# Earlier loads for chunks 2 and 3, zero products in TensorE's waits, products in quarter columns, and results stored by place

## The reference

```
h   = rmsnorm(layernorm(x)) * norm_w;  q, k, v = h Wq, h Wk, h Wv       # 16 heads of 8
lin = causal linear attention, features [1, u, quadratic terms of u],
      u = q Wqf or k Wkf, in chunks of 128 with a running state
win = softmax attention over the key itself and the 64 before it
x1  = x + layernorm(x) + [lin, win] Wout
n   = layernorm(x1);  top 2 of 8 experts by n Wgate + bgate, softmax weights
expert: z = (n W1 + b1)(n W2 + b2);  o = silu(z Wg + bg)(z Wl + bl);  y = o W3 + b3
out = x1 + sum over the token's two experts of weight * y
```

## Time and profile before

| | us |
|---|---|
| median of 3 runs | 412.84 |
| lowest, highest run | 408.07, 413.14 |
| the profiled execution | 410.21 |
| its span, first to last instruction | 408.3 |
| TensorE busy | 343.6 (84%) |
| VectorE busy | 251.6 (62%) |
| GpSimd busy | 219.0 (54%) |
| ScalarE busy | 211.6 (52%) |

### The profile page before, as it was taken

One profiled execution on the slowest core, in us unless ns is written; L12 is line 12 of the kernel. 1 busy time (PEld: TensorE's weight loads), 2 busy tenths in 40 slices (PEclk: granted clock), 3 DMA queues, 4 the chain that ended last, 5 costly groups with the idle time before them and its releaser, 6 DMA issues.

```text
span 408.3 us, 15626 instructions
## 1 busy us (share of the span) xinstructions
PE 343.6 (84%) x5603; PEld 298.1 (73%) x5603; DVE 251.6 (62%) x1001; ACT 211.6 (52%) x574; POOL 219.0 (54%) x368
## 2 busy tenths in 40 slices
PE   0768795699999999999999941699999999999920
PEld 0345584588878788888888830599999999999910
DVE  4665553268986688888887747255555555555515
ACT  0465563366565766676667620355555555555410
POOL 5363554155666577767765554012666655666510
PEclk9999999699999999999999985599999999999985
DMA  7746886878887877554342000223333333333028
GB/s 197 196 123 115 141 218 149 99 166 180 182 188 177 170 134 133 135 128 92 80 92 63 18 32 28 73 60 120 118 122 125 120 127 134 114 119 119 18 67 244
DMA packets 91966, 50.20 MB, mean 123 GB/s; under 512 B 56874, under 2 KB 86220, under 8 KB 91890
## 3 DMA queue, kind: packets, MB, share of 16 engines
q1 hardware_dynamic: 88898, 44.48, 46.0%
q0 software_dynamic: 2272, 4.46, 3.4%
q10 hardware_dynamic: 720, 0.26, 0.3%
HBM read 29.52 MB, written 11.98 MB: 102 GB/s over the span
## 4 chain that ended last, share of the span: by engine, by line
PE 73%; SPq 9%; DMA 6%; DVE 4%; issue 4%; ACT 2%; POOL 1%; DVEq 0%; POOLq 0%; ACTq 0%
PE ps L748 8%; PE ps L754 8%; PE ps L642 6%; PE ps L589 5%; PE ps L720 5%; PE ps L723 4%; PE ps L731 4%; PE ps L638 4%; PE ps L688 4%; PE ps L681 4%; PE ps L601 3%; PE ps L608 3%; SPq L382 3%; SPq L368 3%; PE ps L664 2%
## 5 line engine op out<-in xcount | busy, mean ns | idle before, releaser
L1300 POOL TENSOR_SCALAR_AFFINE_SELECT amat<-amat 128x512 f32<-128x512 f32 x64 | 41.0, 641 | 66.4 <-ACT amat L820 65.7
L1334 POOL DMA_INDIRECT results<-qas,mrowid x39 | 38.2, 979 | 68.1 <-ACT qas L887 68.1
L1103 DVE TENSOR_REDUCE mrow<-ps 128x4 f32<-128x512 f32 x64 | 43.8, 685 | 36.5 <-PE ps L589 36.4
L833 ACT ACTIVATE pmat<-ps 128x512 f32<-128x512 f32 x64 | 38.4, 600 | 54.0 <-PE ps L642 54.0
L1172 DVE SCALAR_TENSOR_TENSOR qas<-ps,bcol,qas 128x128 f32<-128x128 f32 x78 | 26.5, 351 | 34.3 <-ACT qas L893 30.8
L875 ACT ACTIVATE qas<-ps,bcol 128x128 f32<-128x128 f32 x78 | 24.4, 364 | 38.4 <-PE ps L720 38.4
L1182 DVE SCALAR_TENSOR_TENSOR qas<-ps,bcol,qas 128x128 f32<-128x128 f32 x78 | 23.9, 347 | 29.0 <-ACT qas L875 21.7
L820 ACT ACTIVATE amat<-ps 128x512 f32<-128x512 f32 x64 | 38.5, 602 | 1.9 <-PE ps L601 1.7
L1261 POOL DMA_INDIRECT routed<-routed_row,slot x32 | 32.6, 1018 | 12.9 <-issue 5.8
L642 PE MATMUL ps<-minus_ident,mrow 128*128 128x128 bf16 x256 | 36.0, 221 | 0.0
L642 PE MATMUL ps<-minus_ident,mlow 128*128 128x128 bf16 x256 | 35.7, 220 | 0.0
(11 more groups left out here) (170 smaller groups left out, 913.8 us busy)
## 6 DMA issues: line engine op xcount, KB each, us to landing
kv_tok<-w SPq DMA_DIRECT2D x31, 256.0 KB
qa_parts<-wgl SPq DMA_DIRECT2D x12, 256.0 KB, 3.3
ks<-k_parts SPq DMA_DIRECT2D x32, 96.0 KB
qas<-qa_parts SPq DMA_DIRECT2D x32, 96.0 KB
xin<-routed SPq DMA_DIRECT2D x39, 72.0 KB, 1.9
ks<-k_parts SPq DMA_DIRECT2D x32, 64.0 KB
qas<-qa_parts SPq DMA_DIRECT2D x32, 64.0 KB
w<-in_W SPq DMA_DIRECT2D x2, 1024.0 KB
```

The lines of the kernel that those rows point to most:

```text
L833: a_(pmat[:, u % 2].rearrange("p g t -> p (g t)"), ps[:, ST, :], ACT.Exp).then_inc(exp_done, 1)
L1103: v.tensor_reduce(mrow[:, b], ps[:, SQ, :].rearrange("p (a k) -> p a k", k=CH), AX.X, ALU.max).then_inc(max_done, 1)
L1300: q.affine_select(out=amat[:, u % 2], in_=amat[:, u % 2], compare_op=ALU.is_ge, fill=0.0, base=0, pattern=[[0, 4], [1, CH]], channel_multi ...
L1334: q.indirect_dma_start(results, bass.IndirectOffsetOnAxis(mrowid[:, m:m + 1], 0), yw[:, m, :], None, bounds_check=RESULTS - 1, oob_is_err= ...
```

## The change

Stacks 2 and 3 are loaded before the writes of groups 2 and 3: SP's order becomes stack 1, the fill, stack 2, the writes of group 2, stack 3, the writes of group 3, the wait for the writes of groups 1 to 3, stack 4. The weight transfers go out from stack 4 on instead of from stack 3 on.

TensorE gets products of a zeroed buffer `still` with itself, written to a PSUM bank that is then unused: 18 of 512 columns at its start and 4 after the first transposes, 12 and 12 of 128 and 6 and 7 of 512 after the four `post` calls of chunk 16, 6 of 128 and 6 of 512 after the second and third of chunk 17, 30 of 512 before the experts, and 6 of 128 in step -1.

The window scores are made with 32 stationary columns, 16 products a unit. In the experts, ScalarE multiplies b3 by the row's weight into `b3w`, and VectorE multiplies the sum in PSUM by the weight and adds `b3w`. The row numbers of `results` become 16p + c for token p of chunk c, so that a partition's rows lie together, and ScalarE's queue loads the second choice.

```diff
-    vals[:, :, :, 1] = (np.arange(CH)[:, None] + CH * np.arange(NC)[None])[:, :, None] + N * np.arange(TOPK)
+    vals[:, :, :, 1] = (NC * np.arange(CH)[:, None] + np.arange(NC)[None])[:, :, None] + N * np.arange(TOPK)
...
+        BETWEEN = (((12, 128), (12, 128), (6, 512), (7, 512)), ((0, 0), (6, 128), (6, 512), (0, 0)))
+        def half_of_results(k):
+            return results[k * N:(k + 1) * N, :].rearrange("(p c) d -> p c d", p=CH)
...
@@ SP @@
             load_stack(1)
-            for g in range(2, NG):
-                write_parts(g)
             sp.wait_ge(r_in, 16 * N_R)
...
-            for g in range(1, NG):
-                sp.wait_ge(parts_out[g], 16 * WRITES)
...
             for c in range(2, NC):
+                if c == GC:
+                    for g in range(1, NG):
+                        sp.wait_ge(parts_out[g], 16 * WRITES)
                 load_stack(c)
-                for dst, src, got in pieces[c - 3:c - 2] if c >= 3 else ():
+                if c < GC:
+                    write_parts(c)
+                for dst, src, got in pieces[c - GC:c - GC + 1] if c >= GC else ():
                     sp.dma_start(dst, src).then_inc(got, 16)
...
             for g in range(NG):
-                for k in range(2):
-                    lo = k * N + g * GT
-                    sp.dma_start(res[k][:, g * GC:(g + 1) * GC], results[lo:lo + GT, :].rearrange("(c p) d -> p c d", p=CH)).then_inc(res_in[g], 16)
+                sp.dma_start(res[0][:, g * GC:(g + 1) * GC], half_of_results(0)[:, g * GC:(g + 1) * GC]).then_inc(res_in[g], 16)
...
@@ TensorE @@
+            def keep_running(times, cols):
+                for _ in range(times):
+                    mm(ps[:, PHI, 0:cols], still[:, 0:128], still[:, 0:cols], start=True, stop=True)
...
+            pe.wait_ge(still_ready, 1)
+            keep_running(18, 512)
             pe.wait_ge(i_in, 16)
             transposes(0)
+            keep_running(4, 512)
...
@@ window_scores @@
-                    r = WINDOW * (hh % 2)
-                    t = mm(ps[r:r + WINDOW, SQ, (hh // 2) * CH:(hh // 2 + 1) * CH], qs[:, p, h, j * WINDOW:(j + 1) * WINDOW],
-                           ks[:, p, j, h, :], start=True, stop=True)
+                    for z in range(0, WINDOW, 32):
+                        r, at = WINDOW * (hh % 2) + z, j * WINDOW + z
+                        t = mm(ps[r:r + 32, SQ, (hh // 2) * CH:(hh // 2 + 1) * CH], qs[:, p, h, at:at + 32], ks[:, p, j, h, :],
+                               start=True, stop=True)
...
                     post(c, u, c % 2)
+                    keep_running(*BETWEEN[c - NC][u])
...
             pe.wait_ge(r_count, NC)
+            keep_running(30, 512)
             pe.wait_ge(e_in, 16 * N_E)
...
@@ TensorE's step @@
+                if j == -1:
+                    keep_running(6, 128)
...
                     if j > 1:
-                        pe.wait_ge(y_added, j - 1)
+                        pe.wait_ge(y_weighted, j - 1)
...
@@ ScalarE's step @@
-                if on(-1):
-                    m = (k + 3) % 4
-                    act.wait_ge(y_added, j)
-                    act.wait_ge(meta_copied, j)
-                    if j >= 5:
-                        act.wait_ge(y_out[m], 16 * turn(-1))
-                    a_(yw[:, m, :], yb[:, (k + 1) % 2, :], ACT.Copy, scale=mweight[:, m:m + 1]).then_inc(y_weighted, 1)
                 if on(0):
+                    act.wait_ge(meta_copied, j + 1)
+                    if j >= 2:
+                        act.wait_ge(y_weighted, j - 1)
+                    a_(b3w[:, k % 2, :], b3[:, bass.ds(expert(0), 1), :].rearrange("p a f -> p (a f)"), ACT.Copy,
+                       scale=mweight[:, k:k + 1]).then_inc(b3w_ready, 1)
...
@@ ScalarE, at the end @@
+            for k in range(4):
+                act.wait_ge(y_out[k], 16 * ((NT - k + 3) // 4))
+            for g in range(NG):
+                act.dma_start(res[1][:, g * GC:(g + 1) * GC], half_of_results(1)[:, g * GC:(g + 1) * GC]).then_inc(res_in[g], 16)
...
@@ VectorE @@
+            v.memset(still[:], 0.0).then_inc(still_ready, 1)
             v.memset(hT[:, 0:WINDOW], 0.0).then_inc(settled, 1)
...
-                    v.tensor_tensor(yb[:, q, :], ps[:, Y, 0:D], flat(b3[:, bass.ds(expert(-1), 1), :]), ALU.add).then_inc(y_added, 1)
+                    dve.wait_ge(b3w_ready, j)
+                    if j >= 5:
+                        dve.wait_ge(y_out[m], 16 * turn(-1))
+                    v.scalar_tensor_tensor(out=yw[:, m, :], in0=ps[:, Y, 0:D], scalar=mweight[:, m:m + 1], in1=b3w[:, q, :],
+                                           op0=ALU.mult, op1=ALU.add).then_inc(y_weighted, 1)
```

More of the change, by code:

```diff
@@ L230, in build @@
         yw = late2[:, 2560:3072].rearrange("p (a d) -> p a d", a=4)
-        yb = late2[:, 3072:3328].rearrange("p (a d) -> p a d", a=2)
+        b3w = late2[:, 3072:3328].rearrange("p (a d) -> p a d", a=2)
         xin = sb("xin", [CH, 4, ROW])
@@ L237, in build @@
         ps = ctx.enter_context(nc.psum_tensor("ps", [128, 8, 512], F32))
+        still = sb("still", [128, 512], BF16)
         SQ, ST, A, OUT0, OUT1, PHI, KV, TR = range(8)
@@ L244, in build @@
         zeroed = sem("zeroed")
+        still_ready = sem("still_ready")
         wstep, wstep_c = sem("wstep"), sem("wstep_c")
@@ L274, in build @@
         (tx_ready, xT_copied, bcol_ready, x2_ready, x1w_ready, x2_added, z_ready, meta_copied, g_ready, l_ready, silu_done, o_ready,
-         y_ready, y_added, y_weighted) = (sem(n) for n in (
+         y_ready, b3w_ready, y_weighted) = (sem(n) for n in (
              "tx_ready", "xT_copied", "bcol_ready", "x2_ready", "x1w_ready", "x2_added", "z_ready", "meta_copied", "g_ready", "l_ready",
-             "silu_done", "o_ready", "y_ready", "y_added", "y_weighted"))
+             "silu_done", "o_ready", "y_ready", "b3w_ready", "y_weighted"))
         res_in = [sem(f"res_in{g}") for g in range(NG)]
         res_sum, out_sum = sem("res_sum"), sem("out_sum")
+        BETWEEN = (((12, 128), (12, 128), (6, 512), (7, 512)), ((0, 0), (6, 128), (6, 512), (0, 0)))
         TX, X2, X1, G, L, Y = SQ, ST, A, (OUT0, OUT1), (KV, TR), PHI
@@ L893, in step @@
                         a_(sg[:, k % 2, h, :], ps[:, G[h], 0:CH], ACT.Silu, bias=bcol[:, k, 4 + h:5 + h]).then_inc(silu_done, 1)
-            run_steps(act, step)
+            run_steps(act, step, (0,))
+            for k in range(4):
+                act.wait_ge(y_out[k], 16 * ((NT - k + 3) // 4))
+            for g in range(NG):
+                act.dma_start(res[1][:, g * GC:(g + 1) * GC], half_of_results(1)[:, g * GC:(g + 1) * GC]).then_inc(res_in[g], 16)
         @block.vector
@@ L1184, in step @@
                 if on(-1):
-                    q = (k + 1) % 2
+                    m, q = (k + 3) % 4, (k + 1) % 2
                     dve.wait_ge(y_ready, j)
-                    if j > 2:
-                        dve.wait_ge(y_weighted, j - 2)
-                    v.tensor_tensor(yb[:, q, :], ps[:, Y, 0:D], flat(b3[:, bass.ds(expert(-1), 1), :]), ALU.add).then_inc(y_added, 1)
+                    dve.wait_ge(b3w_ready, j)
[3 more added lines that the diff above has]
+                                           op0=ALU.mult, op1=ALU.add).then_inc(y_weighted, 1)
                 if on(1):
```

## The result

| | before | after |
|---|---|---|
| median of 4 runs, us | 412.58 | 406.02 |
| lowest, highest | 408.07, 413.14 | 405.07, 407.34 |
| the profiled execution, its span | 410.21, 408.3 | 405.99, 404.1 |

The account below looks back on a forecast made before the run. TensorE was taken to bound attention and experts, besides idle gaps, half clock, and the head and tail set by other engines and transfers. Terms summed to 19.6: 410.2 - 19.6 = 390.5 us; forecast 386 to 394 (chance 0.60), range 384 to 399.

Parts of the forecast that it names:

- The stacks: SP's queue before attention: the 8.0 us wait and 1.45 at half clock go, a 1.5 us wait comes at chunk 4; -8.0.
- Rival 1: The wait moves: chunk 4 waits some 5 us for its stack, with half clock behind it; 395.5 us, chance 0.17.
- Quarter columns: Window scores in attention: equal strip widths save 0.11 us a unit in 47 units; -5.2 us.
- rivals 2 and 4: 2: each quarter product takes its own slot, 403 us (398.2 at 25 ns), chance 0.06; 4: no overlap, 431, chance 0.03.
- Zeros: Zero products keep TensorE's clock up: -1.7 us at the head, -3.3 after attention, in the first expert tiles.
- Rival 3: Zeros don't hold the clock: no gain at the head or in the experts; 397.5 us, chance 0.08.
- Results of an expert: Experts' weighting moves from ScalarE to VectorE's addition: only the last tile's ScalarE step goes; -0.4 us.
- Results by place: Loading results at the tail in 2 KB instead of 512 B pieces: 6.2 us against 7.4; -1.0 us.

Follow-up runs that it names:

- the wait by group: Changed kernel, but SP waits only for group 1's writes before chunk 4's stack, for groups 2 and 3's behind it; 404.00 us, ratio 0.9826 to the kernel before.
- quarters in two units: Changed kernel with SP's wait for groups 2 and 3 behind chunk 4's stack, and 32-column window scores only in units 0 and 3; 402.04 us, ratio 0.9769.
- the fastest version: Changed kernel with window scores back in 64 columns and SP's wait for groups 2 and 3 behind chunk 4's stack; 400.27 us, again 399.64.

## Why the prediction was wrong, point by point

**The stacks (-8.0).** The wait and its half-clock unit went as summed (the lead grows by 9.7 us from unit 7 to unit 9), and the new wait was 1.8 for my 1.5. That it came so close is partly luck: in the other profiles with this order it was 0, 1.3, 1.4, 2.8 and 3.2. What failed is the rest of that term: the half clock behind the new wait, 1.8 us, and stops of 5.4 instead of 0.8 us. Alone the edit gave 2.1 (408.72 against 410.8). Rival 1 had the place right.

**Quarter columns (-5.2)**, the step that failed outright: alone they cost 4.6 us (415.41 against 410.8, clear of noise), and with the other edits 3.2 (406.02 against 402.85, with intervals of the ratios that just overlap). The slots came as I had read them from L688's row. In chunk 12 (order of time; the earlier trace rows before):

```profile
191.04 0.42 PE L697 MATMUL ps<-amat,v 128*32 128x128 f32 x8
191.28 0.41 PE L704 MATMUL ps<-pmat,v 128*32 128x64 f32 x16
191.50 0.41 PE L605 MATMUL ps<-ks,qas 114*32 114x128 bf16 x16
191.84 0.41 PE L654 MATMUL ps<-qas,ks 114*128 114x64 bf16 x8
```

L704 takes 0.22 for 0.34, L605's sixteen 0.34 as the eight did: 14 and 21 ns a product, the change of width included, so rivals 2 and 4 are out. The Trainium skill, TensorE: Matmul & The Clock Gate, section "Wait — 56ns, not 53.3ns?", has a floor of about 25 ns from start to start; this trace disagrees for strips side by side. (By my own terms, 0.17 less 0.11 in 62 units, that floor would have cost 3.7 us beyond the 5.2 and not 2.5, which makes 399.4 of rival 2's 398.2.) But a chunk still takes 11.40 us late in attention, 11.37 before. Once a chunk, behind the unit with the most short products, this gain is lost:

```profile
205.42 0.64 PE L704 MATMUL ps<-pmat,v 128*32 128x64 f32 x16
206.09 0.43 PE L605 MATMUL ps<-ks,qas 114*32 114x128 bf16 x16
```

0.67 for 0.22; why, no run here tells apart. To that come the stops, and in the profiles compared the wait at chunk 4. I costed products by their slots and took what brings the instructions for free, though the profile of before had the packets on its page and one stop of 0.8 us at 121.75 in its trace.

**Zeros (-1.7, -3.3).** Right in place and, against this execution of the kernel before, in size: in the two executions 1.6 at the head and 2.9 from attention's end to the experts in step. (The kernel without zeros loses more than that, and at the head the luck of the executions is a part of it.) Rival 3 is out: L512's pairs start 0.96 apart, and the clock is 1.00 between 255.83 and 263.81, where it was 0.50. My ground against it, read from the one long wait of the earlier trace rows, doesn't carry over, though: here the clock fell behind a wait of 1.8 us too.

**Results of an expert (-0.4).** Right: 0.5 us of lead between the last L751 and the load of the results.

**Results by place (-1.0).** Nothing: 13.66 us from the first load to the end, 13.65 before. SP's queue and VectorE:

```profile
390.44 1.85 SPq L471 DMA_DIRECT2D ks<-results  x4
...
395.07 0.69 DVE L1232 TENSOR_TENSOR ks<-ks 128x512 f32<-128x512 f32 x1 [7.66 <-DMA ks<-results]
...
400.71 0.69 DVE L1234 TENSOR_TENSOR x_all<-x_all,ks 128x512 f32<-128x512 f32 x1
```

The loads' packets are over 8.8 us after the first issue (I had given 8.5), but group 0's come later (its sum starts at 4.6 us instead of 3.8), as I read it because two queues now fill all groups side by side, and VectorE's eight sums of 0.69 follow each other to the same end.

What stays open: why the moved stacks alone bring more stops, and why the same order makes chunk 4 wait in one kernel and not in another. Executions of one kernel differ: before ranged from 407.0 to 415.2, and one profile each doesn't give the share of chance. In the table, kernels with 16 extra instructions show 7.8 to 9.3 us of stops, the longest execution of the wait by group left out, and those with none 0.8 to 6.3.

## What to carry to other kernels

A program written out at length has its own traffic: look in the profile for idle time put down to nothing within a row of like instructions, number them, and see whether the stops end at the same place in a block. Before a product is split to fill the array better, count its instructions against the rate at which blocks come in while other transfers are heaviest. And a wait that is moved should wait for no more than the work behind it needs; price the half clock behind a new wait as well as the wait.

## What the runs showed of the hardware that I had not expected

- TensorE's instructions come in packets of 16 KB, 256 each, while the program runs, beside the data: 0.9 to 1.9 us each in the changed kernel and up to 2.7 in the other profiles, with stops of up to 2.9 us and, in the longest execution of quarters in two units, 3.2 and 5.2 at a block's end. In fourteen profiles each gap of over 0.7 us between TensorE's instructions within attention, from 49.5 us on, was either at place 193 of 256 or at a wait for a stack.
- TensorE's granted clock fell behind the 1.8 us wait at chunk 4 (mean 0.60 from 89.88 to 94.18) and behind the 2.4 us stop at 96.96 (mean 0.65 from 99.4 to 103.5), but not behind the 1.8 us stop at 52.06: it was 1.00 from 45.35 to 88.05.
- Products of zeros hold the clock: without them the fastest version takes 8 us more (408.36 against 400.27 and 399.64), 2% of its time, with no other work changed.
